# A kernel of two attention layers on one core: order of the fill, and transposed energy two tiles ahead at the end

## The reference

```python
def _L0(x, w_qkv, w_proj, b_proj):       # 8 heads, attention in windows of 32 tokens
    qkv = jnp.einsum('bnwc,cd->bnwd', x, w_qkv)
    ...
    attn = softmax(einsum('bhnqd,bhnkd->bhnqk', q, k) * scale)
    out = einsum('bhnqk,bhnkd->bhnqd', attn, v)
    return einsum('bnwc,cd->bnwd', out, w_proj) + b_proj

def _L1(x, Wq, Wk, Wv, gamma):           # attention over all 1024 tokens
    ...
    energy = jnp.einsum('bid,bjd->bij', k, q)
    attn = jax.nn.softmax(energy, axis=-1)
    return gamma * jnp.einsum('bij,bjc->bic', attn, v)

x = x + _L0(_gn(x), ...)                 # _gn: group norm, 32 groups, per image
x = x + _L1(_gn(x), ...)
```

## Time and profile before

| | us |
|---|---|
| runs | 658.59, 660.24, 663.09 (median 660.24) |
| profiled execution, its own time | 662.23 |
| its span, first to last instruction | 660.40 |
| TensorE busy | 587.2 (89%) |
| VectorE busy | 466.3 (71%) |
| ScalarE busy | 348.3 (53%) |
| GpSimd busy | 204.1 (31%) |
| mean granted TensorE clock | 0.968 of 2.4 GHz |

### The profile page before, as it was taken

How to read it: one execution, slowest core, us unless ns; L and a number is a source line. 1 busy time by engine, 2 the same in 40 slices (tenths; PEclk the granted TensorE clock), 3 DMA queues, 4 the chain that set the end, 5 groups by cost and what they waited for, 6 DMA issues and landing times.

```text
span 660.4 us, 15208 instructions
## 1 busy us (share of the span) xinstructions
PE 587.2 (89%) x5859; PEld 426.5 (65%) x5859; DVE 466.3 (71%) x766; ACT 348.3 (53%) x485; POOL 204.1 (31%) x207
## 2 busy tenths in 40 slices
PE   2898755899999999999999999999999999779777
PEld 2466633457775777667775778578766767547446
DVE  4565477587867787788868787878859784775642
ACT  2763244485268644774278544865288523651461
POOL 7422313202451315320460334231350242212203
PEclk9799977799999999999999999999999999999899
DMA  6112422133224313224223314232322132201001
GB/s 199 55 42 82 113 66 72 40 72 98 73 66 108 99 27 98 77 56 114 52 77 97 96 28 107 81 74 74 92 63 71 34 80 60 78 9 66 17 0 65
DMA packets 39684, 47.53 MB, mean 72 GB/s; under 512 B 6848, under 2 KB 31552, under 8 KB 39632
## 3 DMA queue, kind: packets, MB, share of 16 engines
q1 hardware_dynamic: 34544, 40.85, 23.5%
q10 hardware_dynamic: 4624, 4.98, 2.3%
q0 software_dynamic: 464, 0.98, 0.5%
HBM read 10.09 MB, written 8.39 MB: 28 GB/s over the span
## 4 chain that ended last, share of the span: by engine, by line
PE 67%; DVE 17%; ACT 5%; issue 4%; DMA 4%; SPq 2%; POOL 1%; ACTq 0%; DVEq 0%; POOLq 0%
PE pb L316 9%; PE pb L318 9%; PE pb L317 9%; PE pa L316 6%; PE pa L318 6%; PE pa L317 6%; PE pa L596 4%; PE pb L690 4%; DVE max_neg L1205 4%; PE pa L563 3%; PE pb L668 3%; PE pb L482 2%; DMA diag<-turned 2%; PE pa L482 2%; DVE ast L1100 2%
## 5 line engine op out<-in xcount | busy, mean ns | idle before, releaser
L316 PE MATMUL pb<-v_h,e_h 128*128 128x257 f16 x432 | 118.5, 274 | 0.0
L318 PE MATMUL pb<-v_h,e_l 128*128 128x257 f16 x432 | 117.6, 272 | 0.0
L317 PE MATMUL pb<-v_l,e_h 128*128 128x257 f16 x432 | 117.3, 272 | 0.0
L1205 DVE TENSOR_REDUCE max_neg<-pb 128x1 f32<-128x1024 f32 x61 | 74.1, 1218 | 54.6 <-PE pb L668 54.2
L1220 DVE TENSOR_TENSOR e_l<-e,e_h 128x1024 f16<-128x1024 f32 x64 | 77.9, 1224 | 23.0 <-ACT e L979 21.4
L979 ACT ACTIVATE e<-pb,f_energy 128x1024 f32<-128x1024 f32 x64 | 71.1, 1114 | 15.5 <-PE pb L690 15.5
L989 ACT ACTIVATE qk_h<-pb,y_fac 128x256 f32<-128x256 f32 x53 | 25.1, 473 | 93.7 <-DVE y_fac L1227 93.1
L1478 POOL TENSOR_TENSOR y<-qk_h,y 128x256 f32<-128x256 f32 x63 | 45.3, 726 | 91.5 <-ACT qk_h L989 91.4
L1458 POOL TENSOR_TENSOR xb<-xin,bias 128x2048 f32<-128x2048 f32 x8 | 36.3, 4532 | 120.3 <-DVE x L1185 119.4
L1463 POOL TENSOR_TENSOR before_turn<-before_turn,a_rinv 128x1024 f32<-128x1024 f32 x16 | 30.6, 1916 | 113.2 <-DVE a_rinv L1166 107.8
L978 ACT ACTIVATE e_h<-pb,f_energy 128x1024 f16<-128x1024 f32 x40 | 44.5, 1113 | 19.3 <-PE pb L690 19.3
(11 more groups left out here) (159 smaller groups left out, 1399.2 us busy)
## 6 DMA issues: line engine op xcount, KB each, us to landing
diag<-qkT SPq DMA_DIRECT2D x64, 128.0 KB, 2.4
xin<-in_x SPq DMA_DIRECT2D x15, 512.0 KB, 4.6
diag<-turned SPq DMA_DIRECT2D x60, 128.0 KB, 2.4
turned<-before_turn SPq DMA_DIRECT2D x110, 64.0 KB, 2.0
out<-y SPq DMA_DIRECT2D x24, 256.0 KB, 2.1
...
```

The source lines that it names most:

```text
L316: nc.tensor.matmul(out_ap, lh, rh, start=start, stop=False)
L317: nc.tensor.matmul(out_ap, lh, rl, start=False, stop=False)
L318: return nc.tensor.matmul(out_ap, ll, rh, start=False, stop=stop)
L1205: nc.vector.tensor_reduce(max_neg[:, it:it + 1], energy_banks(b, it).rearrange("p a n -> p (a n)"), X, ALU.max, negate=True).then_inc(b_ma ...
```

## The change

The change moves work and removes none. Each engine's number of instructions stays the same.

End: the fourth `b_project_v` of the last image comes ahead of the row maxima instead of after them; ScalarE's fourth `b_v_high` accordingly stands ahead of `b_rows_in`. In the loop over tiles, the transposed energy of tile jt+2 is issued ahead of the outputs of tile jt instead of behind them.

Fill: on TensorE all four transpose jobs of image 0's block b come together, with the scores of image 1's second chunk behind the averages; v's first half comes ahead of image 2's transposes, and image 2's averages come one energy tile or more later. On ScalarE the exponential of image 1's first chunk comes ahead of image 0's copies, and q/k's high parts and the stack DMAs come ahead of the second exponential. On VectorE the order changes accordingly.

```diff
--- before.py
+++ after.py
@@ -735,6 +735,7 @@
                 b_energy(i, 6, False)
                 b_project_v(i, (2,))
                 b_energy(i, 7, False)
+                b_project_v(i, (3,))
 
             def first(i, b, o, m, f):
 
@@ -797,12 +798,11 @@
 
             def last_second(i):
                 b_max_rows(i)
-                b_project_v(i, (3,))
                 b_energy_T(i, 0)
                 b_energy_T(i, 1)
                 for jt in range(TILES):
+                    if jt + 2 < TILES: b_energy_T(i, jt + 2)
                     outputs_behind(i, (jt,), range(4))
-                    if jt + 2 < TILES: b_energy_T(i, jt + 2)
 
             def second(i, b, o, m, f):
                 if next_to_last(i): return next_to_last_second(i)
@@ -873,24 +873,24 @@
 
             pe.wait_ge(s_ready, 5)
             a_projection(0, True, range(4))
-            transposes("b", 0, (0, 1))
-            a_scores(1, (1,))
-            transposes("b", 0, (2, 3))
+            transposes("b", 0, range(4))
             group_mean("b", 0)
             group_var("b", 0)
+            a_scores(1, (1,))
             pe.wait_ge(s_pool, 6)
             pe.wait_ge(s_ident, 1)
             for c in range(CHUNKS):
                 b_project_qk(0, True, c)
+            b_project_v(0, (0, 1))
             transposes("a", 2, range(4))
-            b_project_v(0, (0, 1))
             b_energy(0, 0, True)
-            b_project_v(0, (2,))
+            b_project_v(0, (2, 3))
+            for it in (1, 2):
+                b_energy(0, it, True)
             group_mean("a", 2)
-            b_project_v(0, (3,))
-            b_energy(0, 1, True)
+            b_energy(0, 3, True)
             group_var("a", 2)
-            for it in range(2, 6):
+            for it in (4, 5):
                 b_energy(0, it, True)
             a_output(1, True, 0)
             b_energy(0, 6, True)
@@ -1000,14 +1000,13 @@
                 if o: b_scaled(i - 1, 6)
                 if m: a_out_high(i + 1)
                 if o: b_scaled(i - 1, 7)
-                if last_image(i): b_v_high(i, range(3))
+                if last_image(i): b_v_high(i, range(4))
 
             def second(i, b, o, m, f):
                 values = b and not image(i, 0) and not last_image(i)
                 if values: b_v_high(i, (0,))
                 if b: b_rows_in(i)
                 if values: b_v_high(i, (1,))
-                if last_image(i): b_v_high(i, (3,))
                 if b: b_exponential(i, 0)
                 if o: store_pair(act, i - 1, 3)
                 if b: b_exponential(i, 1)
@@ -1076,15 +1075,15 @@
             for u in range(2):
                 a_regroup_part(act, a_fx, u, (1, 4, 7))
             a_copy_v(1, (2, 3))
+            a_exponential(1, 0)
             copy_T("b", 0, range(4))
-            a_exponential(1, 0)
             normalise("b", 0)
+            b_qk_high(0)
+            b_stacks(act, b_stack, 0, (1, 3))
             a_exponential(1, 1)
-            b_qk_high(0)
-            copy_T("a", 2, (0, 1, 2))
-            b_stacks(act, b_stack, 0, (1, 3))
-            copy_T("a", 2, (3,))
-            b_v_high(0, range(4))
+            b_v_high(0, (0, 1))
+            copy_T("a", 2, range(4))
+            b_v_high(0, (2, 3))
             normalise("a", 2)
             a_out_high(1)
             all_steps(act, first, second)
@@ -1400,30 +1399,30 @@
             a_out_low(0, 0)
             a_out_low(0, 1)
             a_row_max(1, 0)
-            a_residual(0, range(4))
+            a_residual(0, (0,))
             a_subtract(1, 0)
+            a_residual(0, (1, 2, 3))
             stats("b", 0)
             group_mean("b", 0)
             group_scale("b", 0)
             a_row_sum(1, 0)
             b_norm_split(0)
-            a_maximum(1, 1)
-            b_qk_low(0, (0,))
+            a_row_max(1, 1)
+            b_qk_low(0)
+            a_subtract(1, 1)
+            b_v_low(0, (0, 1))
             a_transpose(1, 0)
-            b_qk_low(0, (1,))
+            b_maximum(0, 0)
+            b_v_low(0, (2, 3))
             a_row_sum(1, 1)
-            b_v_low(0, (0,))
-            stats("a", 2, (0,))
-            b_v_low(0, (1,))
-            b_maximum(0, 0)
-            stats("a", 2, (1,))
+            b_maximum(0, 1)
+            stats("a", 2)
+            b_maximum(0, 2)
             group_mean("a", 2)
-            b_v_low(0, (2,))
+            b_maximum(0, 3)
             group_scale("a", 2)
-            b_v_low(0, (3,))
-            b_maximum(0, 1)
             a_transpose(1, 1)
-            for it in range(2, 8):
+            for it in range(4, 8):
                 b_maximum(0, it)
             b_max_split(0)
             all_steps(dve, first, second)
```

## The result

| | before | after |
|---|---|---|
| median of 6 runs each | 660.81 us (658.59 to 663.09) | 653.47 us (652.63 to 656.03) |
| profiled execution: time, span | 662.23, 660.4 us | 656.03, 654.2 us |
| mean granted clock of TensorE | 0.968 | 0.963 |
| T1 (the first transposes of image 0's second block) to the energy of tile 0 | 24.73 us | 20.45 us |
| energy of tile 0 to the row maxima on TensorE | 22.73 us | 23.71 us |

The ratio is 0.989, with an interval of 0.9865 to 0.9919: 7.3 us less, where the prediction said 10.7 less (660.24 to 649.5). The direction and the range (644.5 to 654.0) hold, the range by only 0.5 us: a third of the sum of 10.9 us was not there. The profiled execution of after was the longest of its six, and the two profiled spans differ by 6.2 us. Another set of 6 runs of the changed kernel gave 653.63 against 661.97, 8.3 us less.

The account below looks back on a forecast made before the run. TensorE bounds the middle, VectorE's last row maximum the fill, its last e_l the tail. Fill 4.2 plus tail 6.7 is 10.9 us, off the profiled 662.2 giving 651.3, off the median 660.24 giving 649.3; stated 649.5, range 644.5 to 654.

Parts of the forecast that it names:

- (d): Whole kernel: the change does nothing, as the middle waits for something else and the tail is bound elsewhere; 659 to 661, chance 0.03.
- (e): Tail: TensorE's clock stays at 1.2 GHz throughout, so the kernel gets slower, 666 us; chance 0.04.
- Rival (c): Tail: only half the gain, as ScalarE and VectorE stall each other through two e buffers; 652.7 to 655, chance 0.07.
- Rival (b): Fill: little gain, value projections of tiles 2 and 3 at 1.2 GHz; 651.8, or 653.5 with late landing; chance 0.15.
- signs of being wrong: TensorE at 0.5 after 630, or over 1 us waiting for diag's DMA before image 1's second output half.
- Fill, steps 1 and 2: Fill, image 0's second block: q/k projection 1.6 us sooner, then stack copies moved ahead; energy 0 4.3 us sooner.
- Fill, step 3: Fill, VectorE's list up to the row maxima: last maximum ends at 120.05 instead of 124.2, fill 4.2 us sooner.
- the landing: Fill: data of image 1's second transpose arrives 4.5 us after that transpose, at 116.3, for the second output half.
- Tail, step 2 with step 1: Tail, last image: value projection early and energy ahead of outputs; outputs 7 start at 638.0, not 644.72, 6.7 us sooner.
- step 1: Tail: fourth value projection moved into the wait for the last maximum; first exponentials 1.6 us sooner, 1.2 at 1.2 GHz.

Follow-up runs that it names:

- earlier transpose: The changed kernel, with VectorE transposing image 1's second chunk before maximum 2 instead of behind maximum 3: 654.47 us, ratio 0.9895 to the kernel before.
- fill alone: The kernel before with only the fill reordered and the old tail kept: 659.93 us against 661.7, ratio 0.9979.
- energy ahead alone: The kernel before with only the last image's transposed energy moved ahead of the outputs, value projection left behind the row maxima: 655.96 us, ratio 0.9922.
- tail alone: The kernel before with both edits of the tail and the old fill: 657.15 us against 661.7, ratio 0.9929.
- value projection alone: The kernel before with only the last image's fourth value projection moved ahead of the row maxima: 662.09 us, ratio 1.0003.
- scores first: The changed kernel, with image 1's 64 score matmuls ahead of image 0's two averages: 655.92 us against 662.17, ratio 0.9916 to the kernel before.
- busy fill: The changed kernel with VectorE's second transpose earlier and 14 unused matmuls behind the fill's energy 2: 653.71 us, ratio 0.988 to the kernel before.

## Why the prediction was right, and where it was too large

**Which stages, and in which direction: right.** The wait of 3.64 us for the stacks fell to 0.23, energy 0 of the tail stands within 0.05 us of the copy, and energy 2 comes ahead of the outputs. Rivals (d) and (e) did not come: TensorE is at 1.00 from 628 on. Rival (c), the tail at half its gain, did not come either. Rival (b), the fill giving little, came half true, by the late landing of diag's data, which it named beside its own mechanism. That mechanism, the value projections of tiles 2 and 3 at the low clock, did not come: the clock fell at 105 us, behind them. Of the signs of being wrong one came, the wait of over 1 us for diag's DMA (1.19), and the row maxima stood at 121.78 where near 120.4 was named. That the median still lies in the range is in part luck: it lies 0.5 us inside the end, and the range was set to take in (b) and most of (c) too.

**Fill, steps 1 and 2: 4.3 us predicted, 3.9 measured.** T1 to energy 0 took 24.7 to 25.1 us in four traces with the old order (mean 24.8) and 20.4 to 21.3 in ten with the new (mean 20.9). The q/k projection came 11.3 us after T1 where 10.5 was worked out: the add in VectorE's chain was held up beside GpSimd (0.3 to 0.5 us), and the second average and its hand-over are slower at the low clock (0.17 us). In the profiled execution this was made up by the stack DMAs, which took 3.45 us from the second qk_hl's end (94.62) to energy 0, where 4.2 was taken over from before.

**Fill, step 3: this is the step that failed.** It predicted 22.8 us from energy 0 to the row maxima, so nothing lost against the 22.73 of before. Measured with the new order: 23.7 to 24.2 in five traces of the unchanged fill (mean 23.9). Two terms were wrong. The first is the landing, put at 4.5 us after the transpose's end: it was 5.4 to 5.9 us until the second half started, in the six traces with the transpose at this place. The rows that I used were 2.0 us from the transpose's end to the last issue and 2.5 for the transfer. The 2.0 held (112.11 to 114.05). The transfer took 3.37, and 3.3 to 3.8 in the other five; in the traces with the old fill or the earlier transpose the last one took 2.4 to 2.6. Everything ahead of it was right: the transpose ended 34.5 us after T1, as worked out (34.6), and with the 4.5 us the second half would have started 0.95 us sooner and energy 0 to the row maxima would have come to 22.8. Why the last transfer is slower in this order no run shows. The second term is the baseline itself. The trace of before held a stretch that other executions of the same order did not. These are TensorE's average of image 2 and the energy pair behind it, with one value projection (twelve matmuls) between them, in before:

```profile
105.64 0.59 PE L489 MATMUL pa<-amv,group_avg 128*128 128x2 f32 x2 [1.04 <-DVE amv L1106]
...
108.61 1.06 PE L668 MATMUL pb<-q_stack,k_stack 96*128 96x512 f16 x2
```

and the same place in the kernel with only the energy ahead, whose fill is the same:

```profile
106.33 0.38 PE L489 MATMUL pa<-amv,group_avg 128*128 128x2 f32 x2 [0.38 <-DVE amv L1106]
...
107.89 0.60 PE L668 MATMUL pb<-q_stack,k_stack 96*128 96x512 f16 x2
```

The average's pair takes 0.59 us in the one and 0.38 in the other, and from there to the energy pair are 2.97 against 1.56 us: the same twelve matmuls once at 1.2 and once at 2.4 GHz. Hence energy 0 to row maxima was 22.7 and 22.9 us in two traces with the old fill, and 21.3 in two others; in the mean 22.1. The old order has the clock on its side here in some executions, and the prediction took over the value of one that had not. With the means, the new order gains some 4 up to energy 0 and loses 1.8 behind it: 2.2 us of the predicted 4.2 (T1 to row maxima 46.9 and 44.7, the latter in the five traces of the unchanged fill). A further part goes in the first segment, from the row maxima of image 0 to those of image 1: 72.7 us in the mean of these five against 72.2 with the old fill. That leaves 1.7, where the fill alone measured 1.4 (0.1 to 2.6).

**Tail, step 2 with step 1: 6.7 us predicted, 6.1 between the two traces, 5.2 between the means.** Row maxima of image 7 to end: 42.9, 42.0 and 41.3 with the old tail (mean 42.1), 36.5 to 37.1 in seven traces with both edits and neither spare matmuls nor the moved cast there (mean 36.8), and 36.5 with the energy ahead alone. Timed, the tail alone gave 4.7 (3.2 to 6.1) and the energy ahead alone 5.2 (3.4 to 7.0). The predicted schedule itself was good to 0.7 us: exponential 3 ends at 627.95 (627.9 predicted), outputs 7 start at 638.51 (638.0), 19.5 us after the copy's end (18.8 predicted). What was mis-sized is step 1, priced at 1.6 or 1.2 and worth nothing. Its cover had been read rightly (the projection's matmuls are hidden in the wait for the last maximum), but not what it did in the old place: with the clock up those matmuls fit into ScalarE's copy of the maxima and cost the path 0.2 us, and they keep TensorE active into the energies. Before's trace had most of them at the low clock, and energy 0 came 2.83 us after the row maxima (620.31); with the fill alone, which has the same tail, they ran at full clock and it came after 1.86, so this too is a matter of the execution.

**The low-clock spell: not in the sum at all.** In nine of the fourteen traces TensorE runs at the low level for 3.4 us somewhere between 562 and 573, in image 6 and in the midst of the loop, and the distance between the row maxima of images 6 and 7 is 60.9 to 61.0 us in these and 59.3 in the five without the spell: 1.6 to 1.7 us. It came with the old fill (tail alone, energy ahead alone) and with the new; it was absent from five, two with the old fill (before, value projection alone) and three with the new (scores first, transpose earlier, busy fill). So it is none of the change's doing, as far as these runs tell. But it makes one pair of traces compare a lucky middle with an unlucky one: without it the spans would differ by 7.9 us and not by 6.2. What brings it on stays open.

**The sum again.** Timed apart the parts make 6.1, as a whole 7.3 and 8.3 in two comparisons, against 10.9. Three terms account for the 3 to 4 us too many: a step worth nothing (1.2 to 1.6), the longer way from energy 0 to the row maxima, the landing above all (23.9 instead of 22.8, 1.1, of which the landing is 0.95 in after), and the baseline of the fill (22.7, where the mean of its four traces is 22.1). The first segment (0.5 in the mean) and VectorE's blocked add (0.3 to 0.5) are of the size of what is left; how it is shared between them the runs don't resolve.
